# Gated cross-attention blocks in fp32 on one core: parts of the row maxima and normalisation of X move from VectorE to GpSimd

## The reference

```
x = x + tanh(g_xattn[0]) * xattn0(layernorm(x), ctx, ctx, mask)
x = x + tanh(g_ffn[0])   * moe(layernorm(x))
x = x + tanh(g_xattn[1]) * xattn1(layernorm(x), ctx)
x = x + tanh(g_ffn[1])   * shift_ffn(layernorm(x))

xattn: q, k, v = heads(x @ Wq + bq), heads(ctx @ Wk + bk), heads(ctx @ Wv + bv)
       attn = softmax(q k^T / sqrt(8)), masked in layer 0
       out  = (attn v, heads joined) @ Wo + bo
layernorm: (x - mean) / sqrt(var + 1e-5)
```

## Time and profile before

| | |
|---|---|
| median of 3 runs | 355.43 us (355.3 to 360.76) |
| the profiled execution | 354.31 us, of which span 352.4 us |
| TensorE busy in the span | 282.6 us (80%), weight loads 206.0 us |
| VectorE busy | 215.5 us (61%) |
| ScalarE busy | 170.3 us (48%) |
| GpSimd busy | 89.4 us (25%) |
| mean granted TensorE clock | 0.915 |

### The profile page before, as it was taken

How to read it: one execution, slowest core, us unless ns; L and a number is a source line. 1 busy time by engine, 2 the same in 40 slices (tenths; PEclk the granted TensorE clock), 3 DMA queues, 4 the chain that set the end, 5 groups by cost and what they waited for, 6 DMA issues and landing times.

```text
span 352.4 us, 7866 instructions
## 1 busy us (share of the span) xinstructions
PE 282.6 (80%) x2970; PEld 206.0 (58%) x2980; DVE 215.5 (61%) x653; ACT 170.3 (48%) x328; POOL 89.4 (25%) x154
## 2 busy tenths in 40 slices
PE   1531869999999999977999988799887777888771
PEld 0110446777777777663366367676765666766651
DVE  3430687567675675662446562875686767848672
ACT  1310226666655665635652613166667566477220
POOL 5210133233251161111001010341432514342140
PEclk9975789999999999996999996958999999899986
DMA  8167447443344431000000042444443341000022
GB/s 234 36 180 185 133 116 216 124 140 118 97 129 112 112 102 32 2 2 0 2 0 0 3 112 92 125 127 114 117 142 106 114 139 63 4 5 2 0 61 60
DMA packets 27663, 30.48 MB, mean 86 GB/s; under 512 B 13699, under 2 KB 24804, under 8 KB 26468
## 3 DMA queue, kind: packets, MB, share of 16 engines
q1 hardware_dynamic: 20366, 27.11, 26.4%
q10 hardware_dynamic: 4188, 2.47, 2.8%
q0 software_dynamic: 3072, 0.40, 0.7%
HBM read 22.43 MB, written 7.14 MB: 84 GB/s over the span
## 4 chain that ended last, share of the span: by engine, by line
PE 56%; DVE 17%; DMA 10%; issue 7%; ACT 5%; POOL 3%; ACTq 1%; DVEq 0%; POOLq 0%
PE bank L991 6%; PE bank L1020 6%; PE bank L972 6%; PE bank L1107 5%; DMA QS<-nmT 5%; PE bank L987 4%; PE bank L968 4%; PE bank L1059 4%; PE bank L1028 3%; DMA QS<-qparts 3%; DVE nmx L450 3%; PE bank L929 2%; PE bank L937 2%; DVE xn L441 2%; DVE st L423 2%
## 5 line engine op out<-in xcount | busy, mean ns | idle before, releaser
L450 DVE TENSOR_REDUCE nmx<-bank 128x4 f32<-128x480 f32 x128 | 81.3, 652 | 46.1 <-PE bank L972 45.8
L770 ACT ACTIVATE P<-bank 120x512 f32<-120x512 f32 x128 | 76.2, 598 | 30.7 <-PE bank L991 29.5
L367 POOL DMA_DIRECT2D QS<-nmT x96 | 47.4, 498 | 140.8 <-ACT nmT L761 140.4
L991 PE MATMUL bank<-QS,KS 75*120 75x128 bf16 x512 | 53.4, 229 | 2.8 <-DMA QS<-nmT 2.3
L972 PE MATMUL bank<-KS,QS 72*128 72x120 bf16 x512 | 51.8, 227 | 4.4 <-DVE nmx L450 3.0
L972 PEld LDWEIGHTS bank<-KS,QS 72*128 72x128 bf16 x512 | 40.1, 104 | 23.3 <-issue 10.5
L991 PEld LDWEIGHTS bank<-QS,KS 75*120 75x120 bf16 x512 | 46.3, 141 | 11.2 <-issue 3.1
L1020 PE MATMUL bank<-P,VS 120*32 120x128 f32 x1024 | 35.4, 280 | 6.6 <-DVE cn L485 4.7
L968 PE MATMUL bank<-MB,IDH 128*128 128x480 bf16 x64 | 24.9, 389 | 14.1 <-DMA QS<-qparts 10.6
L1020 PEld LDWEIGHTS bank<-P,VS 120*32 120x32 f32 x1024 | 27.1, 111 | 9.8 <-ACT P L770 6.0
L441 DVE TENSOR_SCALAR xn<-X,mv,rstd 128x128 f32<-128x128 f32 x64 | 23.0, 479 | 13.6 <-POOL rstd L337 13.6
(11 more groups left out here) (115 smaller groups left out, 441.4 us busy)
## 6 DMA issues: line engine op xcount, KB each, us to landing
KS<-kparts SPq DMA_DIRECT2D x48, 180.0 KB
QS<-qparts SPq DMA_DIRECT2D x42, 192.0 KB
kparts<-kp SPq DMA_DIRECT2D x24, 120.0 KB, 2.8
qparts<-qp SPq DMA_DIRECT2D x21, 128.0 KB, 3.4
QS<-nmT POOLq DMA_DIRECT2D x96, 4.0 KB, 2.6
QS<-qparts ACTq DMA_DIRECT2D x6, 192.0 KB
out<-X SPq DMA_DIRECT2D x4, 256.0 KB, 2.3
X<-in_x SPq DMA_DIRECT2D x3, 256.0 KB, 14.3
```

Of the source, the lines that this page charges most:

```text
L367: po.dma_start(QS[G % 2][STACK + p:STACK + p + 1, k // 2, :, (k % 2) * S:(k % 2 + 1) * S], nmT[Bi % 2][p * H:(p + 1) * H, :]).then_inc(m_l ...
L450: ins = nc.vector.tensor_reduce(nmx[Bi % 2][:, UH * r:UH * r + UH], bank[U % 2][:, 0:UH * SK].rearrange("p (h k) -> p h k", k=SK), AX.X, A ...
L770: nc.scalar.activation(P[Bi % 2][:, hh, :], src, ACT.Exp, scale=SCALE).then_inc(exp_done, 1)
L991: last = mm(o[0:SK, j * S:(j + 1) * S], KS[G % 2][0:ROWS, k // 2, h, (k % 2) * SK:(k % 2 + 1) * SK], QS[G % 2][0:ROWS, k // 2, h, (k % 2) ...
```

## The change

GpSimd takes over two things from VectorE. Its ln_rstd_ goes on to the four tensor_scalar that make xn, so ln_apply is gone, and the next ln on VectorE waits for xn_ok instead of ln_rstd. A new max_parts on GpSimd makes the three parts of the maxima of block s, at the end of what GpSimd does in step s before the due rstd of step 18, behind the row transfers of block s - 1 and the bias on X. It waits for the fourth row maximum of the block, and its four instructions wait on each other by a new semaphore nm_part. VectorE keeps statistics, row maxima, the normalisation of the context (now called normalise) and add_attention. As ln_rstd_ runs ahead of max_rows in a step, the four xn instructions do so too; in the first LayerNorm they stand ahead of the memsets of VS.

```diff
             def ln_rstd_(n):
...
                 po.tensor_tensor(rstd[:, :], ve[:, :], powT[:, :], ALU.pow).then_inc(ln_rstd, 1)
+                phase, g = LN_ORDER[n]
+                if n >= 1:
+                    po.wait_ge(xt_done, n)
+                po.wait_ge(ln_rstd, 2 * n + 2)
+                for i in range(GB):
+                    ins = po.tensor_scalar(xn[:, i, :], X[:, GB * g + i, :], mv[:, i, 0:1], rstd[:, i:i + 1], ALU.subtract, ALU.mult)
+                ins.then_inc(xn_ok, 1)
+
+            def max_parts(Bi):
+
+                i = Bi % 2
+                po.wait_ge(max_done, UNITS * (Bi + 1))
+                if Bi >= 2:
+                    po.wait_ge(nt_done, Bi - 1)
+                po.tensor_copy(nmp[i][:, 0, :], nmx[i][:, :]).then_inc(nm_part, 1)
+                po.wait_ge(nm_part, 3 * Bi + 1)
+                po.tensor_tensor(nmr[:, :], nmx[i][:, :], nmp[i][:, 0, :], ALU.subtract).then_inc(nm_part, 1)
+                po.wait_ge(nm_part, 3 * Bi + 2)
+                po.tensor_copy(nmp[i][:, 1, :], nmr[:, :]).then_inc(nm_part, 1)
+                po.wait_ge(nm_part, 3 * Bi + 3)
+                po.tensor_tensor(nmp[i][:, 2, :], nmr[:, :], nmp[i][:, 1, :], ALU.subtract).then_inc(nm_ok, 1)
...
                     if s < B and s % GB == 1:
                         bias_on_x(L * NG + s // GB)
+                    if s < B:
+                        max_parts(L * B + s)
                     if s == B + 2:
                         ln_rstd_(ln_no(2 * L + 1, NG - 2))
...
-                    v.wait_ge(ln_rstd, 2 * n)
+                    v.wait_ge(xn_ok, n)
...
-            def ln_apply(phase, g):
-                n = ln_no(phase, g)
-                v.wait_ge(ln_rstd, 2 * n + 2)
-                v.wait_ge(ln_var, n + 1)
-                v.wait_ge(dve_c, n_chain[0])
-                if n >= 1:
-                    v.wait_ge(xt_done, n)
-                for i in range(GB):
-                    ins = nc.vector.tensor_scalar(xn[:, i, :], X[:, GB * g + i, :], mv[:, i, 0:1], rstd[:, i:i + 1],
-                                                  ALU.subtract, ALU.mult)
-                ins.then_inc(xn_ok, 1)
...
                         if r == 3 and 4 <= s < B + 4:
-                            parts_and_normalise(None, L * B + s - 4)
-                        if norm and r == 1 and s < B:
-                            ln_apply(*norm)
-                    if s < B:
-                        parts_and_normalise(L * B + s, None)
-                    if s == B + 2:
-                        ln_apply(2 * L + 1, NG - 2)
+                            normalise(L * B + s - 4)
```

More of the change, by code:

```diff
@@ L171, in gated_blocks @@
         v_done = sem("v_done"); v_evac = sem("v_evac"); bo_done = sem("bo_done"); bo_ok = sem("bo_ok")
-        qm_done = sem("qm_done"); max_done = sem("max_done"); nm_ok = sem("nm_ok")
+        qm_done = sem("qm_done"); max_done = sem("max_done"); nm_ok = sem("nm_ok"); nm_part = sem("nm_part")
         nt_done = sem("nt_done"); nt_evac = sem("nt_evac"); m_ld = [sem("m_ld0"), sem("m_ld1")]
@@ L453, in row_max @@
                 ins.then_inc(max_done, 1)
[L455 to L489, removed]
@@ new lines, in normalise @@
+            def normalise(Bn):
+                v.wait_ge(cb_done, Bn + 1)
+                if Bn >= 1:
+                    v.wait_ge(cn_ok, Bn)
+                if Bn >= 2:
+                    v.wait_ge(ct_done, Bn - 1)
+                pv = bank[4][:, :].rearrange("p (h c) -> p h c", c=VW)
+                link(nc.vector.reciprocal(rec[:, :], pv[:, :, HD]))
+                nc.vector.tensor_tensor(cn[Bn % 2][:, :].rearrange("p (h d) -> p h d", d=HD), pv[:, :, 0:HD],
+                                        rec[:, :].unsqueeze(2).broadcast_to([S, H, HD]), ALU.mult).then_inc(cn_ok, 1)
@@ L517, in _ @@
             ln(0, 0)
-            ln_apply(0, 0)
             v.wait_ge(w_in, 64)
@@ L524, in _ @@
             ln(0, 1)
-            ln_apply(0, 1)
             def moe_top(lo, hi):
@@ L666, in _ @@
                     gate_hidden(0, 1)
-                    ln_apply(1, NG - 1)
                     for g in range(NG - 1):
@@ L678, in _ @@
                             ln(2, 0)
-                            ln_apply(2, 0)
                         if g == 2:
@@ L682, in _ @@
                             ln(2, 1)
-                            ln_apply(2, 1)
                     add_moe(NG - 2)
@@ L687, in _ @@
                 else:
-                    ln_apply(3, NG - 1)
                     add_ffn(1)
```

## The result

The changed kernel takes 378.93 us (median of 4 runs, 378.1 to 382.35), the kernel before 357.31 us in the same comparison (4 runs); the ratio is 1.063, 95% interval 1.053 to 1.073. It is slower, where 351.8 us was forecast, with a range of 346.5 to 359.0. The profiled execution took 378.14 us, with a span of 376.2.

The account below looks back on a forecast made before the run. TensorE was taken to bound layer 0's steady part, so gains could come only in layer 1 and at both ends. Terms summed to -3.6 us: median 351.8 us against 355.43, range 346.5 to 359.0.

Parts of the forecast that it names:

- What arrives on GpSimd: Prices of the moved work: one xn 330 ns (bounds 218 and 461), four 1.3 us; parts of the maxima 1.05 us.
- The rival that came true: GpSimd needs 0.68 us per xn, counted nearly one for one in five places: 7 us more, 358.8 us; chance 0.12.
- Plain steps at nothing: In both layers' plain steps VectorE's relief wins nothing, since it only lengthens its wait for the output product.
- a spell of half clock that might go away: Rival: layer 1's half clock from 228 to 241 us goes if earlier maxima close gaps: 2.5 us less, 349.3; chance 0.16.
- Start: First xn on GpSimd ahead of the memsets: first turn moves from 11.69 to 9.50 us, scores with it, -2.2 us.
- First blocks: First blocks of layer 0: without block 1's parts in front, VectorE's bias row and row maximum start earlier, -0.8 us.
- Fourth step of layer 0: xn stands before the row transfers on GpSimd, so rows are issued at 57.1 instead of 56.44 us: +0.7 us.
- The other steps of layer 0: The other three such steps issue rows where TensorE never waits for them: counted at zero.
- Expert stage: TensorE is the chain there and xn is ready before it is wanted: 0.
- Layer 1: First two blocks -0.3 us, fourth and eighth steps nothing, eleventh +0.5 (rows issued later), fifteenth -1.6 (VectorE earlier).
- Tail: Third normalisation of the last phase delays the second difference on GpSimd, +0.5 us; last xn avoids a collision, -0.4 us.
- What leaves VectorE: VectorE loses about 60 us of work and waiting: normalisation 23.0 us plus 13.6 waiting, parts of the maxima 27.

Follow-up runs that it names:

- The copies: The changed kernel with xn made on GpSimd by plain copies of X, normalisation left out, every wait kept: 347.35 us, ratio 0.9816.
- The filled kernels: The changed kernel, and that with only xn moved, each with eight unread TensorE products before ten of sixteen xn turns: 369.19 us (1.05) and 371.65 us (1.0517).
- xn only: The kernel before with the four xn instructions moved to GpSimd and the parts of the maxima left on VectorE: 392.24 us, ratio 1.1006.
- At 602 ns: The changed kernel with xn made by a one-operation tensor_scalar, product with rstd, subtraction of the mean left out: 361.81 us, ratio 1.0168.
- parts only: The changed kernel with the normalisation back on VectorE, so only the parts of the maxima are on GpSimd: 354.2 us, ratio 0.9957.
- memsets late: The kernel before with one wait added, so GpSimd's three memsets of VS come after the first xn: 355.53 us, ratio 0.9894.
- rows late: The kernel before with three scratch tensor_scalar on GpSimd behind each rstd from the third on, xn untouched: 371.45 us, ratio 1.0481.

## Why the prediction was wrong

**The step that failed** is in "What arrives on GpSimd": the price of one xn, 330 ns by the place of a one-input operation between a memset and an operation with two inputs, with 461 as the upper bound. The two lines were right for what they were read from; that an operation with one tensor input must lie under the two-input line was an assumption about a form that no row showed, and it was wrong: the measured 794 ns are 1.7 times the bound and 2.4 times the value taken. The copies show that nothing else was needed for a gain: at 289 ns the kernel takes 0.982 of the time of before (0.9725 to 0.9907), and the forecast, 351.8 against 355.43, was 0.990. The Trainium skill (GPSIMD Engine Reference, § 4.1 Engine selection), whose first half had been made a rival, advises against just this, and the result agrees; its second half, one input at roughly line rate, doesn't hold for this tensor_scalar (0.79 us against 0.34 on VectorE). The copy, 0.28 us, would fit it, but no run here has a copy of this size on VectorE.

**The rival that came true was sized too small.** It had the right mechanism and decided from 0.51 us. By its own working, 794 ns give 351.8 + 20 x 0.464 = 361.1 us; the ratio makes it 377.8. Two things are missing.
- It counted five places. The turn of xn stands in TensorE's own order in the same step, and waited 13 times: 22.0 us, of which the counted four (fourth step of layer 0; eleventh, fifteenth; last xn) hold 9.1. The prediction had asked what stands behind xn on GpSimd (rows, bias, parts) and not who waits for xn itself, beyond the start and the end, since before shows that wait only five times, 4.9 us with both ends (the start's 2.19 among them). "Plain steps at nothing" was right for plain steps; but each layer has five steps with a LayerNorm, and in nine of these ten TensorE waited for xn, 0.74 to 2.74 us.
- It had no price for the clock. The rivals looked at a spell of half clock that might go away; here more of them came, several right behind waits for xn. The filled kernels put 1.3 points (10 us by medians) on it in the changed kernel and 4.9 in the one with xn only; by busy time at half clock the estimate is up to 15.9 us.

**The other terms.** *Start*, -2.2 "for any price up to 0.6 us": with 794 ns xn ends at 10.35, and the first scores start 1.2 us earlier (32.84 for 34.01). At 602 ns the first turn comes at 9.47 and the scores at 30.81, so the bound of 0.6 us was right. With the copies they are at 9.26 and 30.57: the turn gains the 2.4 us that were forecast, the scores 3.4, more than the turn handed on. *First blocks*, -0.8: from block 0 to 1 7.44 us before, 6.58 after, -0.86. *Fourth step of layer 0*, +0.7, was to be a longer wait for the rows, since xn stands in front of them. From block 2 to 4 it is 12.87 us before and 14.35 after, but after has no wait for the rows there at all, only 1.69 us for xn. With the copies it is 14.75, and there TensorE does wait for the rows:

```profile
60.37 0.40 PE L962 MATMUL bank<-IDH,MB 128*120 128x512 bf16 x1 [2.25 <-DMA QS<-nmT]
```

It would be natural to put this +1.9 on xn in GpSimd's queue, and wrong. With the parts only, where xn is made by VectorE and nothing stands in front of the rows, the same place takes 15.76 us:

```profile
55.45 1.53 POOL L381 DMA_DIRECT2D QS<-nmT  x3 [1.06 <-ACT nmT L751]
...
64.73 0.40 PE L977 MATMUL bank<-IDH,MB 128*120 128x512 bf16 x1 [2.64 <-DMA QS<-nmT]
```

From the issue of the rows to the product behind them are 9.3 us here, 7.9 with the copies, and 6.4 before. With the memsets late and nothing moved, this place takes 14.33. What is late is the transfers' landing, and beside it a term of 0.7 us can't be told. Why they land later in these kernels is open.

*The other steps of layer 0*, 0: with the copies blocks 4 to 15 take 73.29 us for 73.72, as forecast; after takes 76.87, and its three waits for xn there come to 3.5 us. *Expert stage*, 0: -1.8 with the copies and +1.2 after, but parts only and rows late have -2.0 and -1.9 as well, and all three have less busy time at half clock there (6.1 to 6.3 us for 10.3), so this isn't xn's.

*Layer 1*, -1.4 in all: -3.8 with the copies, +10.7 after. With the copies the turns of blocks 25 to 27, around the eleventh step, take 12.67 us for 11.87, and those of 28 to 30, around the fifteenth, 10.57 for 12.73: +0.8 and -2.2 for the forecast +0.5 and -1.6. In the changed kernel the stand in the fifteenth step went as said, but a wait for xn took its place. *Tail*, +0.1: -0.5 with the copies, +9.3 after. So the sum of -3.6 us is -9.0 in the trace of the copies: some terms were too small, some of the difference has nothing to do with the change, and the busy time at half clock from block 0 on fell from 33.3 to 21.2 us, which the sum had left to a rival. So the copies bear out the sign of the forecast, and not its sum term by term. That they gain more than was forecast holds for this trace; the ratio's interval (0.9725 to 0.9907) still takes in the forecast's 0.990. That the clock is a reason is inferred from this busy time. (In "What leaves VectorE" the 27 us for the parts should be 32 x 0.8 = 25.6; no term hangs on it.)

**What stays open.** The delay of GpSimd's queue without a late xn cost 4.8%, most of it in one step of layer 1 and the tail; how much of the changed kernel's 6.3% is this delay and how much the late xn itself wasn't measured apart. In its trace the waits point at xn (22.0 us for 4.9 before) and not at the rows (3.7 for 2.6). Why xn alone meets so many more spells at half clock than the full change wasn't tried beyond the filling. Filler products take time of their own, so what they save is rather too low a price for the clock.

## What to carry to other kernels

Before an operation is moved to another engine, measure that very form there, with its operands and its count of operations; a line drawn through other forms was no bound here. Then ask first who waits for the moved result itself, in every step in which it is due, and only then what stands behind it in the new queue; where the waiting engine is TensorE, a wait of 1 to 3 us can be paid twice, since the work behind it may run at half clock. An engine that is 25% busy isn't free capacity for a result with a due time: what counts is the time from the input to the result, and it went from 1.1 to 3.1 us here.

## What the runs showed of the hardware

- GpSimd's tensor_scalar on 128 x 128 fp32 with two operations and two pointers takes 0.79 to 0.80 us, nearly twice a tensor_tensor of that size (0.44) and almost three times a copy (0.28).
- After a wait of 2.08 to 2.74 us, TensorE could run at a granted clock of 0.50 to 0.52 for 6 to 21 us while it was busy 93% and more of the time; after another wait of 2.08 us it stayed at 1.00. Busy time isn't enough to read how fast an engine works: the four small turns are 0.63 us at one clock and 1.09 at the other.
- Putting useless products where TensorE would have waited made a kernel faster by 4.9 points of its ratio (21 us by medians); in a second one it was 1.3 points, within noise, and 10 us by medians.
- VectorE's tensor_scalar stood while GpSimd's memsets ran: the four of the first xn took 4.58 us beside them and 1.11 with the memsets behind. The memsets took the same 4.0 us in both.
- Small row transfers from GpSimd's queue have no fixed time to land: in one and the same step, the work that needs them began 6.4, 7.9 and 9.3 us after their issue in three kernels.
